# Cross-attention of a Perceiver block: Q masked while it leaves PSUM, and restacked by GpSimd's DMA queue

## The reference, cut to what matters

```python
# x (32, 64, 256), context (32, 256, 256), 16 heads of width 16, no scale, no mask
def xattn(queries, keys, values, Wq, Wk, Wv, Wo):
    q = split_heads(queries @ Wq)
    k = split_heads(keys @ Wk)
    v = split_heads(values @ Wv)
    attn = softmax(einsum('bhqd,bhkd->bhqk', q, k))
    return merge_heads(einsum('bhqk,bhkd->bhqd', attn, v)) @ Wo

x = x + xattn(layernorm(x), ctx, ctx, Wq, Wk, Wv, Wo)
x = x + self_attention(layernorm(x))
x = x + feed_forward(layernorm(x))
```

## Time and profile before

| | us |
|---|---|
| median of 3 runs | 704.86 (702.73 to 705.59) |
| the profiled execution | 705.2 |
| its span, first to last instruction | 703.5 |
| start, before the first score | 36.0 |
| quad 0, quad 1, quad 2 (from one rstd to the next) | 44.4, 38.9, 36.7 |
| behind 325.6 (the end of cross-attention and the two other layers) | 377.9 |

### The profile page before, as it was taken

The page is one execution under the profiler, slowest core; times in us unless marked ns, Lnnn a source line. Parts: engine busy times, 40 slices in busy tenths (PEclk is TensorE's granted clock), DMA queues, the critical chain, the costliest instruction groups (busy, mean ns, idle before and its releaser), DMA issues. The chain is left out here.

```text
span 703.5 us, 18671 instructions
## 1 busy us (share of the span) xinstructions
PE 629.0 (89%) x6816; PEld 520.7 (74%) x6816; DVE 464.8 (66%) x981; ACT 384.4 (55%) x1009; POOL 169.5 (24%) x160
## 2 busy tenths in 40 slices
PE   5779588898989898997898899999999999789997
PEld 2567476777777786876587888889897988744497
DVE  3157276777777677677679975666657474657797
ACT  3157376676867677777445142433333252347895
POOL 4340515142333234150002030212112020232000
PEclk9899899999999999999999999999999999999999
DMA  7549455656564636452030000000000000000002
GB/s 239 135 127 315 111 139 121 149 134 149 130 153 113 162 86 150 103 116 62 1 120 3 2 2 1 0 0 0 0 0 0 0 2 2 2 9 0 1 31 91
DMA packets 33865, 52.09 MB, mean 74 GB/s; under 512 B 5376, under 2 KB 13696, under 8 KB 33824
## 3 DMA queue, kind: packets, MB, share of 16 engines
q1 hardware_dynamic: 29280, 42.75, 23.9%
q10 hardware_dynamic: 4352, 8.39, 4.1%
q0 software_dynamic: 192, 0.39, 0.2%
HBM read 17.96 MB, written 2.10 MB: 29 GB/s over the span
## 5 line engine op out<-in xcount | busy, mean ns | idle before, releaser
L562 ACT ACTIVATE Pr<-pS,nmax 128x256 f32<-128x256 f32 x256 | 118.9, 475 | 60.4 <-DVE nmax L658 59.4
L658 DVE TENSOR_REDUCE nmax<-pS 128x2 f32<-128x512 f32 x128 | 87.8, 687 | 76.1 <-PE pS L411 75.2
L332 POOL TENSOR_TENSOR Qst<-Qraw,rows_of 96x1024 fp32r<-96x1024 f32 x32 | 59.9, 1890 | 93.6 <-DMA Qraw<-QSh 90.8
L874 POOL TENSOR_TENSOR a_Pr<-a_Pr,a_rinv 128x512 f32<-128x512 f32 x32 | 32.7, 1044 | 185.8 <-DVE a_rinv L1163 185.8
L421 PE MATMUL pT<-ident,Pr 128*128 128x128 f32 x512 | 77.1, 272 | 0.2 <-ACT Pr L562 0.2
L411 PE MATMUL pS<-Kst,Qst 96*128 96x256 f32 x256 | 59.3, 313 | 9.9 <-ACT Pr L562 4.1
L1043 ACT ACTIVATE a_Pr<-a_Pr 128x512 f32<-128x512 f32 x32 | 20.2, 631 | 76.0 <-DVE a_Pr L1155 76.0
L421 PEld LDWEIGHTS pT<-ident,Pr 128*128 128x128 f32 x512 | 59.2, 140 | 0.4 <-ACT Pr L562 0.4
L569 ACT ACTIVATE PT<-pT 128x512 f32<-128x512 f32 x64 | 38.2, 597 | 32.1 <-PE pT L421 30.5
L411 PEld LDWEIGHTS pS<-Kst,Qst 96*128 96x128 f32 x256 | 39.4, 190 | 20.4 <-ACT Pr L562 9.0
L562 ACT ACTIVATION_READ_ACCUMULATOR Pr<-pS,nmax 128x1 f32 x256 | 52.4, 205 | 0.0
(11 more groups left out here) (266 smaller groups left out, 1880.7 us busy)
## 6 DMA issues: line engine op xcount, KB each, us to landing
Kst<-KSh SPq DMA_DIRECT2D x128, 128.0 KB, 2.5
CT<-ctxT ACTq DMA_DIRECT2D x16, 512.0 KB, 5.0
Kst<-KSl SPq DMA_DIRECT2D x64, 128.0 KB, 2.5
Qraw<-QSh SPq DMA_DIRECT2D x60, 64.0 KB, 2.0
X<-x SPq DMA_DIRECT2D x4, 512.0 KB, 8.7
out<-X SPq DMA_DIRECT2D x8, 256.0 KB, 2.2
Qraw<-QSl SPq DMA_DIRECT2D x30, 64.0 KB, 2.0
raw<-awq SPq DMA_DIRECT2D x1, 1024.0 KB, 7.3
```

The source lines that it names most:

```text
L332: last = pool.tensor_tensor(Qst[r][:, :, :, :, h2, :].rearrange("p j g a q -> p (j g a) q"), Qraw[:, :, r].rearrange("p j g a q -> p j (g ...
L562: act.activation(Pr[c % 2][:, t, :], pS[c % 2][:, t, :], ACT.Exp, bias=nmax[c % 2][:, t:t + 1], accum_out=rsum[par][:, c // 4, 2 * (c % 4) ...
L658: dve.tensor_reduce(nmax[s % 2][:, :], pS[s % 2][:, :, :], AX.X, ALU.max, negate=True).then_inc(maxed, 1)
```

## The change

The mask moves from GpSimd to the eviction of Q. QS gets a further axis for it (`h2`) and doubles. `high` runs two ACT copies, each with one column of `rows_of` as its scale; `low` runs two scalar_tensor_tensor on DVE, (bank times mask) minus high. PE writes Q's projection in another order of columns, with the same matmuls. `Qraw` and `take_q` are gone: `restack_q` writes straight to `Qst[par]`, twelve DMAs for each pair of a quad, 64 KB each, and GpSimd's queue issues them all but six. Each waits for Q's low half and for the scores that read its buffer.

In the first stage SP issues K of pair 0 for three of four row groups and Q for groups 0 and 1, ACT issues K's fourth group behind X's high part, and GpSimd issues Q's groups 2 and 3. The four later weights are no longer issued together: one ahead of K's first restack of quad 0, two behind it, one behind the second. GpSimd makes `rows_of` ahead of the first rstd; DVE splits the first weight and the first context ahead of the statistics; `spare(32)` becomes `spare(12)`.

```diff
-        QS = [sb(f"QS{s}", [P, 2, 2, 2, SQ], F32R) for s in "hl"]
+        QS = [sb(f"QS{s}", [P, 2, 2, 2, 2, SQ], F32R) for s in "hl"]
-        Qraw = sb("Qraw", [96, 4, 2, 2, 2, SQ], F32)
...
-        def restack_q(eng, done, r, quads_taken, groups=range(4)):
+        def restack_q(eng, done, par, r, chunks_done, groups=range(4)):
             after(eng, lo, r + 1)
             apart(eng, waited)
-            after(eng, q_taken, 2 * quads_taken)
+            after(eng, scores, chunks_done)
+            apart(eng, waited)
             for jj in groups:
                 for u, part in enumerate((HI, LO, HI)):
-                    eng.dma_start(Qraw[32 * u:32 * u + 32, jj],
-                                  f32(QS[part][32 * jj:32 * jj + 32])).then_inc(done, 16)
+                    eng.dma_start(f32(Qst[par][32 * u:32 * u + 32, jj]),
+                                  f32(QS[part][32 * jj:32 * jj + 32, par])).then_inc(done, 16)
...
-            restack_k(0, 1, 0)
-            restack_q(sp, qraw_in, 3, 0, (2, 3))
-            restack_k(1, 7, 0)
-
-            for m, w in enumerate(later_weights):
+            def load_later(m):
...
+            restack_k(sp, 0, 1, 0, (0, 1, 2))
+            restack_q(sp, qst_sync, 0, 3, 0, (0, 1))
+            restack_k(sp, 1, 7, 0)
...
-                    restack_q(sp, qraw_in, EV0 + EV * i + 3, i + 1)
-                    restack_k(0, EV0 + EV * i + 5, CHUNKS * (p + 1))
-                    restack_k(1, EV0 + EV * i + 9, CHUNKS * (p + 2))
+                    if first:
+                        load_later(0)
+                    restack_k(sp, 0, EV0 + EV * i + 5, CHUNKS * (p + 1))
+                    if first:
+                        load_later(1)
+                        load_later(2)
+                    restack_k(sp, 1, EV0 + EV * i + 9, CHUNKS * (p + 2))
+                    if first:
+                        load_later(3)
...
-            rstd_of(0)
...
-            restack_q(pool, qraw_pool, 3, 0, (0, 1))
-            take_q(0, 0, 0)
+            rstd_of(0)
+            restack_q(pool, qst_in[0], 0, 3, 0, (2, 3))
             ctx_low(1, 2)
-            take_q(1, 0, 0)
+            restack_q(pool, qst_in[1], 1, 3, 0)
...
-                if not (isinstance(i, int) and i == 0):
-                    take_q(1, i, CHUNKS * 2 * i)
                 if not last:
                     rstd_of(i + 1)
-                if not last:
                     ctx_low(0, 2 * i + 3)
-                    take_q(0, i + 1, CHUNKS * (2 * i + 1))
+                    restack_q(pool, qst_in[0], 0, EV0 + EV * i + 3, CHUNKS * (2 * i + 1))
                     ctx_low(1, 2 * i + 4)
+                    restack_q(pool, qst_in[1], 1, EV0 + EV * i + 3, CHUNKS * (2 * i + 2))
...
-                    spare(32)
+                    spare(12)
...
+                elif kind == "Q":
+                    for h2 in range(2):
+                        last = act.activation(q_target(HI, h2), bank[:, :].rearrange("p (n q) -> p n q", q=SQ), ACT.Copy,
+                                              scale=rows_of[:, h2:h2 + 1])
+                    last.then_inc(hi, 1)
...
                 high(r, r, kind, ahead, part, None)
+                if r == 2:
+                    restack_k(act, 0, 1, 0, (3,))
...
+                elif kind == "Q":
+                    for h2 in range(2):
+                        last = dve.scalar_tensor_tensor(q_target(LO, h2), bank[:, :].rearrange("p (n q) -> p n q", q=SQ),
+                                                        rows_of[:, h2:h2 + 1], f32(q_target(HI, h2)),
+                                                        ALU.mult, ALU.subtract)
+                    last.then_inc(lo, 1)
...
-            dve.wait_ge(x_in0, 16)
-            statistics(0, 0)
             split_w(0)
             dve.wait_ge(ctx_hi, 1)
             dve.tensor_tensor(CS[LO][:, :, :], CT[0][:, :, :], f32(CS[HI][:, :, :]), ALU.subtract).then_inc(ctx_lo, 1)
+            dve.wait_ge(x_in0, 16)
+            statistics(0, 0)
             normalize(0)
```

More of the change, by code:

```diff
@@ L251, in q_restacked, with restack_k @@
         def q_restacked(eng, quads):
-            eng.wait_ge(qraw_pool, RESTACK // 2)
-            eng.wait_ge(qraw_in, RESTACK * quads - RESTACK // 2)
-        def restack_q(eng, done, r, quads_taken, groups=range(4)):
+            eng.wait_ge(qst_in[0], RESTACK * quads - RESTACK // 2)
+            eng.wait_ge(qst_in[1], RESTACK * quads)
+        def restack_q(eng, done, par, r, chunks_done, groups=range(4)):
             after(eng, lo, r + 1)
             apart(eng, waited)
-            after(eng, q_taken, 2 * quads_taken)
+            after(eng, scores, chunks_done)
+            apart(eng, waited)
             for jj in groups:
                 for u, part in enumerate((HI, LO, HI)):
-                    eng.dma_start(Qraw[32 * u:32 * u + 32, jj],
-                                  f32(QS[part][32 * jj:32 * jj + 32])).then_inc(done, 16)
+                    eng.dma_start(f32(Qst[par][32 * u:32 * u + 32, jj]),
+                                  f32(QS[part][32 * jj:32 * jj + 32, par])).then_inc(done, 16)
+        def restack_k(eng, b, r, chunks_done, groups=range(4)):
+            after(eng, lo, r + 1)
+            apart(eng, waited)
+            after(eng, scores, chunks_done)
+            for jj in groups:
+                for u, part in enumerate((HI, HI, LO)):
+                    eng.dma_start(f32(Kst[b][32 * u:32 * u + 32, jj:HP:4, :]),
+                                  f32(KS[part][32 * jj:32 * jj + 32, :, :])).then_inc(kst_in[b], 16)
         block = ctx.enter_context(nc.Block())
@@ L284, in _ @@
                 load_x(n)
-            def restack_k(b, r, chunks_done):
-                after(sp, lo, r + 1)
-                apart(sp, waited)
-                after(sp, scores, chunks_done)
-                for jj in range(4):
-                    for u, part in enumerate((HI, HI, LO)):
-                        sp.dma_start(f32(Kst[b][32 * u:32 * u + 32, jj:HP:4, :]),
-                                     f32(KS[part][32 * jj:32 * jj + 32, :, :])).then_inc(kst_in[b], 16)
-            restack_k(0, 1, 0)
-            restack_q(sp, qraw_in, 3, 0, (2, 3))
-            restack_k(1, 7, 0)
-            for m, w in enumerate(later_weights):
+            def load_later(m):
+                w = later_weights[m]
                 sp.dma_start(raw[:, m, :].rearrange("p (k n) -> p k n", n=w.shape[1]),
                              w.rearrange("(k p) n -> p k n", p=P)).then_inc(raw_in[m], 16)
+            restack_k(sp, 0, 1, 0, (0, 1, 2))
+            restack_q(sp, qst_sync, 0, 3, 0, (0, 1))
+            restack_k(sp, 1, 7, 0)
             def body(i, last):
                 p = 2 * i
+                first = isinstance(i, int) and i == 0
                 if not last:
-                    restack_q(sp, qraw_in, EV0 + EV * i + 3, i + 1)
-                    restack_k(0, EV0 + EV * i + 5, CHUNKS * (p + 1))
-                    restack_k(1, EV0 + EV * i + 9, CHUNKS * (p + 2))
+                    if first:
[7 more added lines that the diff above has]
+                        load_later(3)
             steps(sp, body)
@@ L325, in ctx_low @@
                 pool.tensor_tensor(CS[LO][:, :, :], CT[b][:, :, :], f32(CS[HI][:, :, :]), ALU.subtract).then_inc(ctx_lo, 1)
-            def take_q(r, quad, chunks_done):
-                q_restacked(pool, quad + 1)
-                after(pool, scores, chunks_done)
-                for h2 in range(2):
-                    last = pool.tensor_tensor(
-                        Qst[r][:, :, :, :, h2, :].rearrange("p j g a q -> p (j g a) q"),
-                        Qraw[:, :, r].rearrange("p j g a q -> p j (g a) q"),
-                        rows_of[0:96, h2:h2 + 1].unsqueeze(2).unsqueeze(3).to_broadcast([96, 4, 4, SQ]), ALU.mult)
-                    if h2 == 0:
-                        last.then_inc(q_half, 1)
-                last.then_inc(q_taken, 1)
-            rstd_of(0)
             for u in range(4):
```

18 lines of the change are left out of this document (10 added, 8 removed).

## The result

| | before | after |
|---|---|---|
| median, on one chip, 4 runs each | 703.80 us (701.41 to 705.59) | 680.66 us (678.91 to 682.20) |
| the profiled execution, its span | 705.2, 703.5 | 680.65, 678.8 |
| granted clock, mean | 0.981 | 0.994 |

The ratio is 0.9674 (95% interval 0.9651 to 0.9697): 23 us faster in the medians and 24.6 in the profiled executions, where 17.1 were forecast.

A forecast was written before the change was run, and what follows sets the result against it. Time was taken to be lost before the first score and in a TensorE hole in quad 0; 7.6 + 9.6 + 2.0 - 2.1 = 17.1 us off 705.2 gave 688 us, range 683.5 to 699.

The forecast's parts named there:

- the start: Up to the first scores and next K projection: 6.0 plus 1.6 us gained, together 7.6, bounds 5.5 to 9.
- the loop: Seven quads: longer Q eviction on VectorE costs 0.3 us a quad, 2.1 us in all, bounds 0 to 9.8.
- X arrives as before, so XN is as before: First stage: normalized rows come no sooner; weight splits still end at 14.7 us, Q is projected at 17.8.
- I leave its clock there as it was: First scores: with 12 warm-up matmuls TensorE idles about 2 us where it idled 2.96, so its clock is unchanged.
- Quad 0: TensorE's 8.4 us wait for the low context goes, plus 1.2 us of slow clock: 9.6 us gained, bounds 7 to 10.
- the hole: In quad 0, 71.2 to 79.6 us holds one matmul; Q's restack stood behind four 1 MB weights on SP.
- Quad 1: K no longer behind twelve Q restacks on SP, its wait goes: 2.0 us gained, bounds 1.6 to 2.2.
- has over 15 us until its use: Quad 0's moved weights: SP's K restack for the second pair has over 15 us before it is needed.
- Slow issues beside a busy VectorE: Rival, chance 0.1: GpSimd's DMA issues in the loop wait for VectorE instructions, rstd comes late; 726 or 698 us.
- The drag: Rival: the longer eviction reaches TensorE in full, or half the start's gain with 0.8 us a quad; 693.7 to 695.8; shared chance 0.25.
- The hole moves only: Rival: quad 0's low context is late again by half the hole, 692.9 us; chance 0.25 shared with the drag.
- No change: Rival, chance 0.05: Q's landing, not mask or queue, set both the start and quad 0; about 703 us.

The follow-up runs named there:

- experiment 3: Changed kernel with one edit each: VectorE's old first-stage order, 682.83 us; all of K's first restack on SP, 687.44 us; 32 warm-up matmuls, 684.69 us.
- experiment 4: Five filler matmuls per body: changed kernel 680.20 us, kernel before 700.79; changed kernel repeated unchanged 683.24; changed kernel with fillers and warm-up of 24, 678.66.
- Experiment 1: Changed kernel with all four later weights ahead of K's first restack of quad 0, 692.31 us; kernel before with only the weights spread, 700.33 us.
- Experiment 2: Changed kernel with Q's loop restack all on SP, 699.94 us; with four more GpSimd DMA issues ahead of rstd, 684.33 us; with eight, 697.29 us.

## Why the prediction was right or wrong

The measured time lies under the range by three terms: the start was 2.0 us more than its 7.6, the loop did not pay its 2.1, and quad 5 and what lies behind it gave 3.8 us of which the sum had nothing.

**The start: 9.6 us for 7.6.** The mechanism was right and the term too small; two steps in it failed. "X arrives as before, so XN is as before": X was there 0.5 us sooner (8.32 for 8.79), and between X and XN lies rstd on GpSimd, which the new order on VectorE halved (0.72 for 1.55 us, experiment 3). XN was at 10.66 for 12.20, the weight splits ended at 13.2 where I had 14.7, and the Q projection was at 16.61 where I had 17.8; by the run with VectorE's old order (17.20) about half of that 1.2 us comes from the order. The other is the speed of the Q projection itself: from its first matmul to its eviction 16.61 to 18.33 is 1.7 us, against 2.9 in the earlier trace rows, of which I took the old value; it now ran at the full clock. Q's low half was thus ready at 21.04, 2.4 us sooner than I had it, and the scores came at 28.14, 1.9 sooner than my 30.0. They came behind SP's last issue of Q, and not behind GpSimd's, as I had it: with more of K on SP and GpSimd's issues where they were, the scores were 0.8 us later (experiment 3). The last microsecond gained at Q's low half brought next to nothing, because SP was at K's restack until 22.0. The eviction (1.4 us longer), the two restack queues, and the low context in time for the K projection went as worked out. "I leave its clock there as it was" held: the K projection behind the scores ran in part at 1.2 GHz before as well (0.77 us for its first matmul in the earlier trace rows, 0.40 at full clock), and from the first score to vare, without the wait of 1.61 us, it was 7.7 us before and 7.6 after. What that clock costs is 1.6 us, and the warm-up of 24 kept it (experiment 4). The 9.6 lies above my upper bound of 9, and the vare that it rests on differs by 1.3 us from one execution of this start to the next.

**Quad 0: 9.4 us for 9.3, and the mechanism.** GpSimd's twelve issues, the low context ahead of its projection, the slack of about 1 us (made at 61.0 for 61.9), the clock behind it: each where I had put it or near. Experiment 1 adds what the prediction did not say clearly: neither half does it. With K alone behind four weights the hole was back at 7.3 us, and with Q alone on SP's queue K was late by 4.3.

**Quad 1: 1.6 for 1.7, the number by luck.** The wait for K of the earlier trace rows, 31 us into the quad, is gone as forecast. But the sentence on the moved weights, that SP's K restack for the second pair "has over 15 us until its use", does not hold: 15 us lie between its first issue and its use, 8.1 between its last issue and its use, and beside the weights that K took 7.6 us to land, so TensorE waited 0.67 us for it at 83.91, 13 us into the quad. The clock has no part in it: it is 1.00 throughout. In the seven profiled executions that have this wait (0.67 to 1.57 us) quad 1 takes 36.6 us and the wait; in this one it was the smallest. With the weights early that wait is not there (K landed in 3.7 to 5.1 us), but another, of 0.94 us, is; no run has the weights elsewhere, so that they are the cause is argued and not shown.

**What the loop pays: 0 for 2.1.** The term was mis-sized, and in quads 2 and 3, where it can be read, its sign was wrong. VectorE does work 0.7 us longer per quad and ScalarE as much, but TensorE's rows of quad 2 are later by only 0.06 us behind the Q eviction (the score at 26.87 for 26.81, counted from vare), and 0.02 of it is there ahead of the eviction. And K's operand for the coming quad, with nothing of Q ahead on SP, is there sooner:

```profile
155.20 0.61 SPq L292 DMA_DIRECT2D Kst<-KSl  x1
...
157.80 0.50 PE L411 MATMUL pS<-Kst,Qst 96*128 96x256 f32 x2
```

```profile
133.16 0.60 SPq L273 DMA_DIRECT2D Kst<-KSl  x1
...
137.08 0.41 PE L406 MATMUL pS<-Kst,Qst 96*128 96x256 f32 x2
```

These are the last issue of K and the first score that reads it, in quad 2 before and after. Before, 2.6 us lay between, and K took 2.4 to 2.5 to land (medians of the quad): the score came with nothing to spare, though the trace names no wait there. Now there are 3.9, for 3.1 to land, and the score comes 0.15 us sooner in the quad (29.02 for 29.17) although the rows ahead of it are later; all that follow in the quad are 0.24 sooner. I had looked for K's lateness in quads 0 and 1 alone. That K was the cause here is read from these rows; no run took it apart.

**Quad 5 and behind: 3.8 us that nothing in the forecast held.** They are TensorE's clock, which the sum has nowhere in these stretches. Quad 5 is 1.5 us shorter with fillers in the kernel before as well (experiment 4). Behind it the trace of before loses 3.4 us to the clock (0.8, 0.9 and 1.7) and the profiled execution of after 1.8 (0.16 of 10.9, at 254.1): 1.6 of the 2.1. Which execution has how many such stretches is chance, as far as the runs show. The 0.5 left would fit the last two quads, at the 0.2 to 0.3 of the others. The dips stand in the trace of before, and I read the clock of 79.6 to 89.7 only. Seeing them I would have had to widen the range at its low end: 688 less the 5.1 us of these four rows is 683, and the low end has the other bounds still to come.

**The rivals.** Slow issues beside a busy VectorE: 498 ns in the median of 124, 746 at most, no effect; VectorE here reads PSUM on nearly every line, so that by the page cited in the prediction (the Trainium skill, SBUF — State Buffer, "SBUF: two separate sides") no slower issue was due, and none came. Experiment 2 shows the rest of the rival's mechanism to be sound, that a late rstd reaches the end: eight issues more, and the time rises by 14 us. The drag: the eviction reaches TensorE with at most 0.06 of 1.4 us. The hole moves only: with both parts in, no more of it than the 0.67 us in quad 1; with either part alone it moved to K. No change: refuted by 23 us.

One term which the forecast lacked takes something back: GpSimd stops once.

```profile
212.78 0.98 POOL L264 DMA_DIRECT2D Qst<-QSh  x2 [2.92 <-issue]
...
217.70 0.24 POOL L328 TENSOR_SCALAR vare<-mv 128x2 f32<-128x2 f32 x1
```

It comes in the quad that was 36.8, so that vare was late by what the pause exceeded the slack, 0.3 us; the cost is 0.4 us in all.

## What to carry to other kernels

A queue is a position in line before it is bandwidth: when a transfer is moved off a shared queue, ask which one is next behind the same obstacle. Here each part alone brought nothing or 3.2 us in quad 0, and both 9.4. Where large transfers are spread out, count the slack of those beside them from their last issue, not from their first. Where an engine takes over issues, count what is queued behind them until its next deadline: four 0.5 us issues inside 2.6 us of slack were covered, eight cost more than they overran. Compare single stages of two traces only by more than what the same code differs by: here 1.3 us at the first vare. Before costing a change, read the clock of every stretch of the kernel before; stretches of low clock that it does not cause come and go between runs, and a few fillers in a short wait of TensorE, with a longer warm-up, gained 4.6 us and made the time steady.

## What was not expected of the hardware

- GpSimd's arithmetic on a tile of two columns took 1.55 us beside a VectorE subtraction of two SBUF tiles and 0.72 us without one, with nothing changed but the order of VectorE's work.
- GpSimd paused for 2.2 to 2.9 us after exactly 128 DMA issues, in each of the ten profiled executions that had so many, whether the 129th came at 183 us (with eight extra issues a quad) or at 223, and whichever tile it wrote. It follows the count, not the time or the tile. With Q on SP, GpSimd issued 18 and did not pause. What it waits for is not shown.
- With 4 MB ahead on SP's queue 128 KB took 9.9 us to land, while 64 KB on GpSimd's queue took 5.9 at the same time and 2.1 in quad 2.
- Waits of 1.3 and 0.9 us, 2 us apart, cost the full clock in some quads and not in others of the same execution (10 of 32), each time some 1.7 us of work.
- The same start, with a wait of 2.5 to 2.8 us ahead of the scores, lost the clock in five executions and kept it in two; it costs 1.6 us at vare.
